# Two plans of a two-layer kernel: 52 instead of 32 unread products on TensorE, and the first six gathers moved from the expert stage into the plan's block

## What is computed

```
# layer 0                                   # layer 1
assign = argmax(x @ centroids.T, axis=1)    probs = softmax(xt @ Wg); each expert marks its top T/E tokens
h = relu(layernorm_e(xs) @ w1[e].T + b1[e])   tok2exp = argmax over the marking experts, or over all if none marks
y = alpha * (xs + h @ w2[e].T + b2[e]) + (1 - alpha) * xs
                                            out = weight * (gelu(xt @ W1[e]) @ W2[e])
x = x + gb * y                              x = x + gb * out
```

## Time and profile before

| | us |
|---|---|
| median of 3 runs | 1241.12 |
| lowest, highest | 1239.78, 1241.14 |
| the profiled execution | 1241.38 |
| its span (first to last instruction) | 1239.6 |

### The profile page before, as it was taken

The page is one execution under the profiler, slowest core; times in us unless marked ns, Lnnn a source line. Parts: engine busy times, 40 slices in busy tenths (PEclk is TensorE's granted clock), DMA queues, the critical chain, the costliest instruction groups (busy, mean ns, idle before and its releaser), DMA issues. The chain is left out here.

```text
span 1239.6 us, 28644 instructions
## 1 busy us (share of the span) xinstructions
PE 997.7 (80%) x10307; PEld 844.8 (68%) x10308; DVE 680.2 (55%) x1555; ACT 435.6 (35%) x1179; POOL 346.5 (28%) x308
## 2 busy tenths in 40 slices
PE   4477888877389999999994888999877624899996
PEld 1255556655288999999993677777765413799995
DVE  2356676666452444444453057888979467344442
ACT  0222222221003444454452476777654200032221
POOL 0001111111112222222212054555555100345552
PEclk9699888887669999999997899999976655799998
DMA  7774411111165322222210556666632160134441
GB/s 256 244 268 124 150 34 34 34 35 34 68 273 159 95 86 86 85 93 86 84 56 22 108 97 122 127 135 131 120 83 72 63 271 1 64 112 145 135 134 43
DMA packets 132105, 135.36 MB, mean 109 GB/s; under 512 B 73748, under 2 KB 122006, under 8 KB 130604
## 3 DMA queue, kind: packets, MB, share of 16 engines
q1 hardware_dynamic: 120780, 90.80, 26.1%
q0 software_dynamic: 11232, 43.27, 11.0%
HBM read 96.21 MB, written 44.77 MB: 114 GB/s over the span
## 5 line engine op out<-in xcount | busy, mean ns | idle before, releaser
L868 PE MATMUL psall<-rows 128*128 128x128 f32 x1872 | 221.9, 275 | 2.2 <-DVE rows L923 2.2
L868 PEld LDWEIGHTS psall<-rows 128*128 128x128 f32 x1872 | 215.3, 192 | 2.7 <-issue 2.6
L880 PE MATMUL psall<-whi,rows 128*128 x624 | 141.0, 379 | 0.0
L923 DVE COPY rows<-wlo 128x2048 f32 (+1 forms) x78 | 74.9, 961 | 110.8 <-PE psall L868 107.5
L833 POOL DMA_INDIRECT x<-ffn_rows,tok_i x78 | 82.4, 1056 | 182.3 <-DVE rows L942 142.2
L880 PEld LDWEIGHTS psall<-whi,rows 128*128 128x128 f32 x624 | 115.7, 190 | 14.1
L470 POOL TENSOR_TENSOR whi<-whi 128x1024 f32<-128x1024 f32 x8 | 18.8, 2348 | 298.3 <-DVE rows L367 298.3
L1159 DVE STREAM_TRANSPOSE whi<-whi 32x512 f32<-32x512 f32 x128 | 89.8, 701 | 9.0 <-POOL whi L1127 7.7
L980 ACT ACTIVATE rows<-psall,rows 128x128 f32<-128x128 f32 x312 | 84.6, 382 | 9.6 <-PE psall L868 5.9
L1229 ACT ACTIVATE whi<-psall 32x512 f32<-32x512 f32 x128 | 75.1, 587 | 31.3 <-PE psall L1340 28.2
L880 PE MATMUL psall<-wlo,rows 128*128 x312 | 73.6, 379 | 0.0
(11 more groups left out here) (206 smaller groups left out, 1795.4 us busy)
## 6 DMA issues: line engine op xcount, KB each, us to landing
ffn_rows<-mod_rows SPq DMA_DIRECT2D x2, 4096.0 KB
wlo<-in_W SPq DMA_DIRECT2D x2, 4096.0 KB, 17.0
x<-in_x SPq DMA_DIRECT2D x1, 4096.0 KB, 22.7
whi<-mod_rows SPq DMA_DIRECT2D x4, 1024.0 KB, 14.6
ffn_rows<-rows SPq DMA_DIRECT2D x8, 512.0 KB
ffn_rows<-x SPq DMA_DIRECT2D x8, 512.0 KB
wlo<-attn_rows SPq DMA_DIRECT2D x32, 128.0 KB, 3.4
v_turn<-wlo SPq DMA_DIRECT2D x32, 128.0 KB, 3.4
```

What stands on the lines that cost most here:

```text
L868: last = eng.matmul(b_up[t.par][f // 4][:, (f % 4) * P:(f % 4 + 1) * P], w_now[:, c, f * P:(f + 1) * P], inT[t.par][:, c * P:(c + 1) * P], ...
L880: last = eng.matmul(b_dn[t.par][:, 0:D], hidT[t.par][:, f * P:(f + 1) * P], w_down[:, bass.ds(e, 1), f, :].rearrange("p o n -> p (o n)"), ...
L923: eng.tensor_copy(w_now, w_up[:, bass.ds(e, 1)].rearrange("p o c n -> p (o c) n")).then_inc(e_["w"], 1)
```

## The change

Three edits. First, both plans issue 52 instead of 32 unread products ahead of the turning. Second, DVE's write of `tok_i` raises a new semaphore `p_tok`, and DVE no longer waits for that write before it copies `slot_w`. Third, a new function `fetch_first` on POOL waits for `p_tok` and issues the first six fetches at the end of POOL's list in the plan's block; the expert stage's loop leaves them out.

```
         def keep_tokens(eng, ch):
-            ch.do(eng.tensor_scalar(tok_i[:, :], ps[2][:, 0:NTILE], float(T), None, ALU.add))
+            eng.tensor_scalar(tok_i[:, :], ps[2][:, 0:NTILE], float(T), None, ALU.add).then_inc(p_tok, 1)
             ch.do(eng.tensor_copy(slot_w[:, :], ps[2][:, NTILE:2 * NTILE]))
...
+        def fetch_first(eng, layer):
+
+            eng.wait_ge(p_tok, layer + 1)
+            for j in range(DEEP):
+                eng.indirect_dma_start(x[:, j * 3 * D:(j + 1) * 3 * D], None, fin_d[layer],
+                                       bass.IndirectOffsetOnAxis(tok_i[:, j:j + 1].bitcast(U32), 0),
+                                       bounds_check=T, oob_is_err=False).then_inc(s_in[j], 16)
...
                 prefix_pe(eng, onehot).then_inc(p_pre, 1)
-                hold_clock(eng, 32)
+                hold_clock(eng, 52)
                 invert_pe(eng, 0).then_inc(p_inv, 1)
...
             def _(eng):
                 invert_pool(eng, 0)
+                fetch_first(eng, 0)
...
                     for s in range(NTILE + DEEP):
-                        if s < NTILE:
+                        if DEEP <= s < NTILE:
                             fetch_rows(s)
                         if s >= DEEP:
                             put_rows(s - DEEP)
```

More of the change, by code:

```diff
@@ L711, in keep_tokens @@
         def keep_tokens(eng, ch):
-            ch.do(eng.tensor_scalar(tok_i[:, :], ps[2][:, 0:NTILE], float(T), None, ALU.add))
+            eng.tensor_scalar(tok_i[:, :], ps[2][:, 0:NTILE], float(T), None, ALU.add).then_inc(p_tok, 1)
             ch.do(eng.tensor_copy(slot_w[:, :], ps[2][:, NTILE:2 * NTILE]))
-        p_one, p_pre, p_exp, p_held, p_low, p_inv = (sem("p_" + n) for n in "one pre exp held low inv".split())
+        p_one, p_pre, p_exp, p_held, p_low, p_inv, p_tok = (sem("p_" + n) for n in "one pre exp held low inv tok".split())
+        s_in = [sem(f"s_in{i}") for i in range(DEEP)]
+        def fetch_first(eng, layer):
[4 more added lines that the diff above has]
+                                       bounds_check=T, oob_is_err=False).then_inc(s_in[j], 16)
         cx = Carve(x)
@@ L768, in wait_some @@
                 eng.wait_ge(s, count * each)
-        s_in = [sem(f"s_in{i}") for i in range(DEEP)]
         class Tile:
@@ L1439, in _ @@
                 invert_pool(eng, 1)
+                fetch_first(eng, 1)
         def waits1(eng, who):
```

## The result

The changed kernel takes 1246.43 us (median of 10 runs, 1242.24 to 1249.62), the kernel before 1236.70 us (median of 10 runs, 1233.10 to 1241.14). The ratio is 1.0077 with a 95% interval of 1.0057 to 1.0097: **slower by 9.5 us, between 7 and 12**. The forecast was slower by 3.5 us, 1244.6 us on the base of 1241.12 that was known then. The direction is right and the time lies in the range, but the loss is 2.7 times the forecast one.

What follows compares the result with a forecast made beforehand. The prediction took the slack-free chain of PE's turning, `tok_i`, block end, 20 unread products and transposes as the bound. Turning -12.1, gathers ahead of the drain +15.8, products -0.2 gave +3.5 us: 1244.6 us, 8-in-10 range 1242 to 1251.

Steps and rivals of the forecast that it cites:

- The turning: PE's map turning in both plans: 52 products keep the clock up, 7.2 us each, gain 6.6 + 5.5 = 12.1 us.
- rivals C and D: Turning loses the clock some 4 us in, 1250.0 us, chance 0.12 (C); only one plan loses it, 1247.4 us, 0.12 (D).
- The gathers' own time: Six gathers on POOL at the plan block's end: first starts 0.82 us after `tok_i`, all six take 7.5 us.
- The release: Block's end behind POOL's gathers: drain, report and release take 0.35 us, without waiting until the last rows have landed.
- The 20 products: Unread products opening each expert stage: start at the low clock again, 6.5 us each, -0.2 us together, give or take 1.5.
- The sum: Whole kernel: -12.1 + 15.8 - 0.2 = +3.5 us, +0.3%, added to the median 1241.12: 1244.6 us.
- narrow range: The forecast's own range from gather trains, unread products and clock phases of attention 1: 1242.3 to 1247 us.
- wide one: The range for 8 in 10, leaving out B, the poor half of C and the lowest of A: 1242 to 1251 us.
- Rival B: Block's end: the drain lets queued indirect DMAs pass, so the 15.8 us go: 1226 us, chance 0.06.
- A: The forecast itself, 1244.6 us, chance 0.70, with 0.17 of it counted as same, 0.53 as slower and 0.01 as faster.

Runs made afterwards that it cites:

- the sixth experiment: Changed kernel with the lists of plan and expert stage in one block, so no block end between gathers and the 20 products: 1219.72 us, ratio 0.9863 against before.
- the fourth experiment: Kernel before with 52 products, fetches in the stage, plus one plain POOL transfer per plan, 768 KB in plan 0, 8 KB in plan 1: ratio 0.9925.
- the seventh experiment: Changed kernel without the stage's 20 unread products, with 56 behind the turning in the plan instead: 1234.43 us, ratio 0.9966 against before.

## Why the prediction was right in direction and short in size

**The turning: right.** Forecast 7.2 us at full clock and ends 6.6 and 5.5 us earlier; measured 7.34 and 7.27 us, and 6.6 and 5.6 us earlier, counted from the plan's first unread product. That the products of 78 columns hold a clock which they never raised was taken from rows that lay near, and it held in both plans of all seven kernels with 44 or 52 products ahead; rivals C and D did not happen.

**The gathers' own time: nearly right.** Forecast 0.82 us to the first start and 7.5 for the six; measured 0.90 and 7.72, 0.83 and 7.61. The first gather took 1.20 and 1.09 us with DVE idle, not 1.0. Of the excess of before, 0.6 and 0.2 us, which I laid wholly to DVE's copy, DVE's part is thus 0.4 in stage 0 and 0.1 in stage 1; the rest belongs to a first gather after a pause. That DVE's copy does hold a gather up is seen apart in the sixth experiment, where the third of a train took 1.58 us beside it.

**The release: wrong, and this is the step that failed.** The prediction put drain, report and release at 0.35 us and said of a drain that waits for the rows: "That the drain lasts until the last rows have landed I exclude". It excluded it by SP's drain, 0.12 us with a transfer in flight. That row holds for SP and says nothing of POOL: SP's transfer went on after SP's drain, while POOL's drain in the fourth experiment ends with the landing at both sizes. Measured from the last gather's end to PE's start: 3.94 and 4.19 us, 3.6 and 3.8 more than put in. The cost of a plan, 12.6 us from `tok_i` to PE less the 0.77 of before, is 11.8 and 11.9 us instead of 7.9, 23.7 together instead of 15.8.

**The 20 products: right.** 6.5 us each forecast, 6.17 and 6.46 measured, -0.6 us instead of -0.2. They started at the low clock again, as forecast. That they cover nothing behind the block's end, the seventh experiment confirms.

**The sum.** -12.2 + 23.7 - 0.6 = +10.9 us by the traces, +9.5 by the timing. With the term as it was measured, the prediction's own working gives +11.4. The direction was forecast and came about by the mechanism named, a train of gathers ahead of the block's end. That the time of 1246.4 us lies only 1.8 above the forecast 1244.6 is luck: the base, 1241.12 from three runs, came out as 1236.70 from ten, 4.4 us lower, and hid most of the 6 us by which the forecast loss was too small. As a loss, 9.5 us lies outside the prediction's own narrow range (+1.2 to +5.9) and inside its wide one only near the upper end (+0.9 to +9.9).

Rival B (the release does not wait for the gathers) put the time 15 us below before. The sixth experiment, where there is no release to wait for, measured -17 us.

**Two slips in the recorded working, on which nothing hangs.** The low slices 31 to 34 of the earlier trace rows lie ahead of plan 1's turning, in slice 35, which reads 7. And the three parts into which A's 0.70 is split add up to 0.71.

## What to carry to other kernels

Before a DMA that POOL issues is moved ahead of a block's end, count its landing and not only its issue: here all engines waited for what POOL had issued last, and the 20 covering products behind the block's end came on top. A transfer that should start early and overlap needs a semaphore of its own and no barrier behind it. And a change of two halves should be tried by halves: one of these was worth -14 to -17 us, the other +21.

## What the runs showed of the hardware

- POOL's drain ends when POOL's own transfers have landed (8 KB: 1.9 us after the start; 768 KB: 4.5; in the changed kernel the drain ended 4.7 and 4.9 us after the start of the last gather). SP's drain took 0.12 us at 341.3, with a load of 1024 KB under way that SP had issued at 340.93 and that landed 23.8 us after its start. POOL's drain did not wait for this load of SP either: it ended at 353.96. Only POOL and SP were seen in this; ACT issued no transfer.
- The products of 78 columns ran for 13.9 us at 0.50 without a rise, and for 7.3 us at 1.00 without a fall. In which of the two they ran went with the pause ahead of them: with none, 1.1 or 1.7 us the clock held; with 4.3 us it was low when they began, and with 3.8 us (plan 1 before) they began at 1.00 and fell after 0.55 us.
- The same code between two plans took 663.9 to 671.3 us in ten executions, and single timings of the kernel before ranged over 11 us on these chips. Part of it can be seen: of two executions of the kernel with 52 products alone, the stretch took 3.4 us longer in the second (669.4 against 666.0), and 1.6 of these are the first 32 products of stage 0, 3.74 us at a granted clock of 1.00 in the one and 5.36 in the other, whose clock was 0.58 from 368.8 to 372.2. Where the rest comes from, no run here isolated.
